# The end of an image-prompt cross-attention kernel, written out for its last two tiles

## The reference

```python
q = heads(hidden_states @ W_q)
probs_t = softmax(einsum(q, k_t) * attn_scale)
text_out = einsum(probs_t, v_t)
attn_scores = einsum(q, k_ip) * attn_scale
qsem = l2norm(einsum(probs_t, text_ehs))
sem = einsum(qsem, l2norm(ip_ehs))
fused = attn_scores + 0.5 * sem
probs_ip = softmax(fused) * spatial_mask
out = (text_out + einsum(probs_ip, v_ip)) @ W_out + b_out + hidden_states
```

## Time and profile before

| what | value |
|---|---|
| median of 3 runs | 332.41 us (332.4 to 334.32) |
| span of the profiled execution, first to last instruction | 330.6 us |
| PE busy | 307.7 us (93%) |
| DVE busy | 285.0 us (86%) |
| ACT busy | 278.2 us (84%) |
| POOL busy | 208.3 us (63%) |

### The profile page before, as it was taken

The page is one execution under the profiler, slowest core; times in us unless marked ns, Lnnn a source line. Parts: engine busy times, 40 slices in busy tenths (PEclk is TensorE's granted clock), DMA queues, the critical chain, the costliest instruction groups (busy, mean ns, idle before and its releaser), DMA issues.

```text
span 330.6 us, 9014 instructions
## 1 busy us (share of the span) xinstructions
PE 307.7 (93%) x2290; PEld 290.9 (88%) x2290; DVE 285.0 (86%) x1966; ACT 278.2 (84%) x1210; POOL 208.3 (63%) x422
## 2 busy tenths in 40 slices
PE   3999899898999999999999999999999999999974
PEld 3788878798999899989999999989998999899863
DVE  5666757899899989999999989998999899989973
ACT  3836688989999898989898989898989989898941
POOL 3053326686958686767776777768786967664241
PEclk9999999999999999999999999999999999999999
DMA  6960003001202020202011020212021201000001
GB/s 200 343 179 0 1 13 82 3 1 32 60 22 63 29 64 20 63 27 59 27 28 42 25 61 22 60 34 60 22 61 33 61 21 62 30 22 21 23 21 61
DMA packets 15131, 17.02 MB, mean 51 GB/s; under 512 B 2592, under 2 KB 14536, under 8 KB 15080
## 3 DMA queue, kind: packets, MB, share of 16 engines
q1 hardware_dynamic: 15080, 16.44, 16.5%
HBM read 10.55 MB, written 5.24 MB: 48 GB/s over the span
## 4 chain that ended last, share of the span: by engine, by line
PE 48%; DVE 24%; ACT 24%; issue 2%; DMA 1%; SPq 0%
PE gv_ps L902 13%; ACT e_sb L528 12%; PE mi_ps L865 9%; DVE place_ctxT L682 7%; PE mi_ps L937 7%; PE et_ps L889 6%; PE sc_ps L881 5%; DVE negmax L674 3%; ACT place_w L541 2%; DVE attnT_low L759 2%; ACT xh L504 2%; DVE q_rest L662 2%; DVE qs L665 2%; ACT place_ctxT L537 2%; ACT xh L506 2%
## 5 line engine op out<-in xcount | busy, mean ns | idle before, releaser
L528 ACT ACTIVATE e_sb<-sc_ps,negmax 128x60 f32<-128x60 f32 x640 | 150.2, 339 | 16.1 <-DVE negmax L674 15.2
L902 PE MATMUL gv_ps<-tab,place_w 128*128 128x162 f32 x640 | 115.1, 302 | 0.6 <-ACT place_ctxT L537 0.6
L682 DVE CUSTOM_DVE_ANT_0 place_ctxT<-gv_ps,e_sb 128x60 f32<-128x60 f32 x640 | 99.7, 210 | 13.8 <-PE gv_ps L902 11.7
L902 PEld LDWEIGHTS gv_ps<-tab,place_w 128*128 128x128 f32 x640 | 94.0, 190 | 1.8 <-issue 1.0
L881 PE MATMUL sc_ps<-km,qs 128*128 128x256 f32 x320 | 77.4, 324 | 0.0
L889 PE MATMUL et_ps<-ident,e_sb 128*128 128x128 f32 x320 | 63.2, 279 | 8.8 <-ACT e_sb L528 8.0
L541 ACT COPY place_w<-et_ps 128x256 f32<-128x256 f32 x160 | 66.5, 416 | 0.3 <-PE et_ps L889 0.3
L674 DVE TENSOR_REDUCE negmax<-sc_ps 128x4 f32<-128x240 f32 x160 | 63.2, 395 | 0.0
L889 PEld LDWEIGHTS et_ps<-ident,e_sb 128*128 128x128 f32 x320 | 40.9, 139 | 18.3 <-ACT e_sb L528 16.9
L682 DVE DVE_READ_ACCUMULATOR2_ANT quad<- 128x1 f32 x640 | 51.7, 81 | 0.0
L537 ACT COPY place_ctxT<-gv_ps 128x84 f32<-128x84 f32 x160 | 43.7, 273 | 6.5 <-DVE quad L682 6.4
(11 more groups left out here) (158 smaller groups left out, 583.5 us busy)
## 6 DMA issues: line engine op xcount, KB each, us to landing
x_nat<-in_x SPq DMA_DIRECT2D x16, 320.0 KB, 3.1
out<-place_w SPq DMA_DIRECT2D x32, 160.0 KB, 1.8
place_ctx<-in_ctx SPq DMA_DIRECT2D x4, 256.0 KB, 4.0
place_w<-in_L_xattn_W_v SPq DMA_DIRECT2D x1, 640.0 KB, 7.3
place_w<-in_L_xattn_W_k SPq DMA_DIRECT2D x1, 640.0 KB, 8.6
place_w<-in_L_xattn_W_k_ip SPq DMA_DIRECT2D x1, 640.0 KB, 10.3
place_w<-in_L_xattn_W_v_ip SPq DMA_DIRECT2D x1, 640.0 KB, 10.4
place_ctxT<-in_L_xattn_W_out SPq DMA_DIRECT2D x1, 640.0 KB
```

The costliest lines, as they stand in the source:

```text
L528: last = nc.scalar.activation(e_sb[:, slot, TOK * j:TOK * j + T], sc_ps[:, bank, TOK * j:TOK * j + T], ACT.Exp, bias=negmax[:, slot, j:j + 1])
L682: last = v.tensor_tensor_reduce(out=junk[:, u % 2, j, 0:T], in0=gv_ps[:, u % 2, TABW * j:TABW * j + T], in1=e_sb[:, u % ERING, TOK * j:TOK ...
L902: last = mm(gv_ps[:, u % 2, 2 * TABW * r:2 * TABW * r + 2 * TABW], eT[:, u % TRING, P * r:P * r + P], tab[:, b % 2, h:h + 2, :].rearrange( ...
```

## The change

What it does, part by part. A constant `PLAIN` (30) is the first of two tiles whose small steps leave the slots:

1. For tiles 30 and 31 `rnorm` is made on POOL with a power of -0.5 (128x20) ahead of the text part of `mixed`, in place of the logarithm and exponential on ACT.
2. For these tiles `semn`, `fused`, the maximum and `ipd` are a straight piece of DVE code, `centre(t)`: after slot 157 for tile 30, and after the last slot for tile 31. Sum, reciprocal and weighing are another, `normalize_and_weigh(t)`, after slot 158 and at the end. The weighing is one DVE instruction (`weigh`) in place of two on POOL, for tile 29 too. ACT's `ipe` of tile 30 stands after slot 157, that of tile 31 at the end.
3. `ENDING` puts the transposes of tile 29 in slot 158 (from 159) and its products in 159 (161), those of tile 30 in 160 (164) and 161 (166). Tile 31's text transposes come right after slot 160.
4. The image-prompt chunk of tile 31 is copied in fp32 and multiplied in one fp32 product, in place of a rounded half, a remainder and three fp32r products.
5. The residuals of tiles 29 and 30 are added at the end of DVE's program, after `xl`, the remainder of tile 31's text chunks.

```diff
+    PLAIN = ALL_TILES - 2
+        ENDING = {-2: ("at", -3), -1: ("o", -3), 0: ("at", -2), 1: ("o", -2)}
         def misc_task(u):
+            if u >= ALL_UNITS - 2:
+                kind, t = ENDING.get(u - ALL_UNITS, ("", 0))
+                return kind, 0, ALL_TILES + t
...
@@ GpSimd, tile(t)
+                if PLAIN <= t - 1 < ALL_TILES:
+                    pool.wait_ge(quadc_made, t)
+                    g.tensor_tensor(rnorm[:, b1], quadc[:, b1], neg_half[:], ALU.pow).then_inc(rnorm_made, 1)
                 if 0 <= t - 1 < ALL_TILES:
                     pool.wait_ge(rsum_made, t)
                     g.tensor_tensor(mixed[:, (t - 1) % ARING, 0:C].rearrange("p (h d) -> p h d", d=D), fin[:, b1, :, NIP:NIP + D],
...
-                if 0 <= t - 2 < ALL_TILES:
+                if 0 <= t - 2 < PLAIN - 1:
                     pool.wait_ge(iprec_made, t - 1)
...
-                if 0 <= t - 1 < ALL_TILES:
+                if 0 <= t - 1 < PLAIN:
                     pool.wait_ge(rnorm_made, t)
...
@@ ScalarE
+            def weights(t):
+                act.wait_ge(ipd_made, t + 1)
+                nc.scalar.activation(ipe[:, t % 2], ipd[:, t % 2], ACT.Exp).then_inc(ipe_made, 1)
-            for u in range(ALL_UNITS + GROUPS + 1):
+            for u in range(ALL_UNITS + 2):
                 slot(u)
+                if u == ALL_UNITS - 3:
+                    weights(PLAIN)
+            weights(PLAIN + 1)
             act.wait_ge(last_done, 1)
             nc.scalar.copy(last_attnT[:, 0:2 * P], LAST_ATTN[:, 0:2 * P]).then_inc(last_hi, 1)
             act.wait_ge(last_done, 2)
-            nc.scalar.copy(last_attnT[:, 2 * P:3 * P], LAST_IP).then_inc(last_hi, 1)
+            nc.scalar.copy(last_ip[:], LAST_IP).then_inc(last_hi, 1)
...
@@ VectorE
+                    if t - 2 == PLAIN - 1:
+                        weigh(t - 2)
...
+            def weigh(t):
+                dve.wait_ge(iprec_made, t + 1)
+                v.scalar_tensor_tensor(
+                    out=mixed[:, t % ARING, C:C + IPCOLS].rearrange("p (h n) -> p h n", n=NDIF), in0=ipe[:, t % 2, :, 0:NDIF],
+                    scalar=mask_sb[:, t % TILES:t % TILES + 1], in1=iprec[:, t % 2].unsqueeze(2).to_broadcast([P, HEADS, NDIF]),
+                    op0=ALU.mult, op1=ALU.mult).then_inc(pip_made, 1)
+            def centre(t):
+                n, steps = t % 2, 3 * (t - PLAIN)
+                dve.wait_ge(fin_copied, GROUPS * (t + 1))
...
+                dve.wait_ge(guard_made, t + 1)
+                v.tensor_tensor(quadc[:, n], quad[:, n], guard[:, n], ALU.max).then_inc(quadc_made, 1)
+                v.reciprocal(rsum[:, n], ssum).then_inc(rsum_made, 1)
+                dve.wait_ge(rnorm_made, t + 1)
+                v.tensor_tensor(semn[:, n], fin[:, n, :, 0:NIP], rnorm[:, n].unsqueeze(2).to_broadcast([P, HEADS, NIP]),
+                                ALU.mult).then_inc(end_step, 1)
...
+            def normalize_and_weigh(t):
+                n = t % 2
+                dve.wait_ge(ipe_made, t + 1)
...
+            for u in range(ALL_UNITS + 1):
                 slot(u)
+                if u == ALL_UNITS - 3:
+                    centre(PLAIN)
+                if u == ALL_UNITS - 2:
+                    normalize_and_weigh(PLAIN)
+            centre(PLAIN + 1)
+            attnT_lows(PLAIN)
+            normalize_and_weigh(PLAIN + 1)
             dve.wait_ge(last_hi, 1)
...
-            dve.wait_ge(last_hi, 2)
-            v.tensor_tensor(last_attnT_low[:, 2 * P:3 * P], LAST_IP, last_attnT[:, 2 * P:3 * P].bitcast(F32),
-                            ALU.subtract).then_inc(last_lo, 1)
+            for t in (PLAIN - 1, PLAIN):
+                add_residual(mi_ps[:, misc_bank(("o", 0, t)), 0:C], t)
             add_residual(LAST_OUT, ALL_TILES - 1)
@@ TensorE, last_products and the loop
-                pe.wait_ge(last_lo, 2)
-                for k in range(len(steps) - 3, len(steps)):
-                    last = mm(LAST_OUT, steps[k][0], steps[k][1], start=False, stop=k == len(steps) - 1)
-                last.then_inc(out_done, 1)
+                pe.wait_ge(last_hi, 2)
+                mm(LAST_OUT, last_ip[0:OUT_ROWS], u_nat[0:OUT_ROWS, B - 1], start=False, stop=True).then_inc(out_done, 1)
+            for u in range(ALL_UNITS + 1):
                 slot(u)
+            last_attn_transposes()
+            slot(ALL_UNITS + 1)
+            slot(ALL_UNITS + 2)
             last_products()
```

More of the change, by code:

```diff
@@ L268, in xattn_kernel @@
         MISC_ORDER = [("x", 0, 0), ("x", 1, 0), ("q", 0, 0), ("q", 1, 0), ("q", 2, 0), ("v", 0, 0), ("x", 0, 1), ("x", 1, 1)]
-        MISC_ORDER += [misc_task(u) for u in range(ALL_UNITS + UNITS) if misc_task(u)[0]]
+        MISC_ORDER += [misc_task(u) for u in range(ALL_UNITS + GROUPS) if misc_task(u)[0]]
         def misc_bank(task):
@@ L489, in tile @@
                                     ALU.subtract).then_inc(ipd_made, 1)
-            for t in range(ALL_TILES + 2):
+            for t in range(ALL_TILES + 1):
                 tile(t)
@@ L613, in slot @@
                     exps(u + LEAD)
-                if j == 3 and 0 <= t - 1 < ALL_TILES:
+                if j == 3 and 0 <= t - 1 < PLAIN:
                     act.wait_ge(lnq_made, t)
@@ L618, in slot @@
                     copy_eT(u + TLEAD)
-                if j == 0 and 0 <= t - 2 < ALL_TILES:
+                if j == 0 and 0 <= t - 2 < PLAIN:
                     act.wait_ge(ipd_made, t - 1)
@@ new lines, in centre @@
+            def centre(t):
+                n, steps = t % 2, 3 * (t - PLAIN)
+                dve.wait_ge(fin_copied, GROUPS * (t + 1))
+                ssum = fin[:, n, :, FINW - 1]
+                v.scalar_tensor_tensor(out=guard[:, n], in0=ssum, scalar=EPS * EPS, in1=ssum,
+                                       op0=ALU.mult, op1=ALU.mult).then_inc(guard_made, 1)
+                dve.wait_ge(guard_made, t + 1)
[4 more added lines that the diff above has]
+                                ALU.mult).then_inc(end_step, 1)
+                dve.wait_ge(end_step, steps + 1)
+                v.tensor_tensor(fused[:, n], semn[:, n], sip[:, t % SRING], ALU.add).then_inc(end_step, 1)
+                dve.wait_ge(end_step, steps + 2)
+                v.tensor_reduce(ipmax[:, n], fused[:, n], AX_X, ALU.max).then_inc(end_step, 1)
+                dve.wait_ge(end_step, steps + 3)
+                v.tensor_tensor(ipd[:, n], fused[:, n], ipmax[:, n].unsqueeze(2).to_broadcast([P, HEADS, NIP]),
+                                ALU.subtract).then_inc(ipd_made, 1)
@@ new lines, in normalize_and_weigh @@
+            def normalize_and_weigh(t):
+                n = t % 2
+                dve.wait_ge(ipe_made, t + 1)
+                v.tensor_reduce(ipsum[:, n], ipe[:, n], AX_X, ALU.add).then_inc(ipsum_made, 1)
+                dve.wait_ge(ipsum_made, t + 1)
+                v.reciprocal(iprec[:, n], ipsum[:, n]).then_inc(iprec_made, 1)
+                weigh(t)
+            for u in range(ALL_UNITS + 1):
+                slot(u)
+                if u == ALL_UNITS - 3:
+                    centre(PLAIN)
+                if u == ALL_UNITS - 2:
+                    normalize_and_weigh(PLAIN)
@@ L1087, in slot @@
                     table_products(u)
-            for u in range(ALL_UNITS + 2 * GROUPS - 2):
-                if u == ALL_UNITS + GROUPS + 1:
-                    last_attn_transposes()
+            for u in range(ALL_UNITS + 1):
                 slot(u)
+            last_attn_transposes()
+            slot(ALL_UNITS + 1)
+            slot(ALL_UNITS + 2)
             last_products()
```

10 lines of the change are left out of this document (5 added, 5 removed).

## The result

The changed kernel takes 346.86 us (median of 4 runs, 346.37 to 348.71) against 333.37 us for the kernel before in the same comparison: a ratio of 1.0426, 95% interval 1.039 to 1.0463. It is slower, as forecast, but by 13.5 us where 6.1 were forecast; it lies above the range.

The account below looks back on a forecast made before the run. The prediction took the end to be bound by the order in which engines wait for each other, none being full: 5.0 us up to quad(159) plus 1.1 after it, 332.4 + 6.1 = 338.5 us, range 334 to 344.

Parts of the forecast that it names:

- one power: POOL's 128x20 power for `rnorm`, tiles 30 and 31: taken as 1.2 us each, between bounds 0.59 and 7.4.
- end of power to end of `semn`: DVE's `semn` ends 0.14 us after POOL's 0.74 us text multiplication: 0.88 us after the power, instead of about 0.24.
- end of `semn` to end of `ipd`: `fused`, the maximum and `ipd` on DVE with their self-waits: 0.73 us in the sum.
- quad(156) to quad(159): DVE, ACT and PE queues stop at tile 30's power; quad(159) ends at 324.44, 5.0 us later than before.
- quad(159) to the last residual: Tile 31's small steps, then tile 30's products and the last chunk: 9.99 us against 8.92, 1.07 later.
- whole end, over before: Both parts of the end, before and after quad(159): 5.0 + 1.1 = 6.1 us longer.
- The order of the waits: DVE waits at `semn`, ACT at `ipe`, PE for fin(156); tile 30's products wait for tile 29's residual.
- The hold: POOL's text multiplication slows DVE's `semn` beside it: 0.64 us, counted twice, 1.28 in the sum.
- The first rival: The power is paid by the column: 342 us at 3 us each, 351 at 7.4; power above 3 us, chance 0.10.
- The second rival: The power is short and POOL's multiplication doesn't hold `semn`: 335.5 to 337.2 us, chance 0.13.
- The fp32 product: Tile 31's last chunk: one 0.78 us product replaces three taking 0.72 and a remainder; saves 0.29 us.
- The third rival: At DVE's wait for `rnorm`, little is held and shorter steps decide: 331.6 us; not slower or smaller costs, chance 0.15.

Follow-up runs that it names:

- e2b: Changed kernel plus useless TensorE transposes (40, 8, 36 and 18 at four places in the end) to keep TensorE busy; 343.26 us, ratio 1.029.
- e3: Changed kernel with tile 29's residual moved into tile 31's centering, in VectorE's wait for the power; 345.31 us, ratio 1.0357.
- e6: Changed kernel with POOL's `mixed` of both last tiles waiting for `ipd`, so it can't run beside `semn`; 346.24 us in one run.
- e1: Changed kernel without the power: ScalarE makes `rnorm` for the last two tiles by logarithm and exponential; 342.42 us, ratio 1.0243.
- e9: e1 plus useless TensorE transposes (12, 8, 8 and 16 at four places in the end); 337.25 us, ratio 1.0105.
- e8: Kernel before with one fp32 last-chunk product, tiles 30 and 31 weighed on VectorE, three neighbours exchanged; no power; 330.93 us, ratio 0.9913.
- e10: e9 with e3's move, POOL's `mixed` of tile 30 held until `ipd`, 6 transposes instead of 16 before tile 30's products; 334.52 us, ratio 1.0032.
- e2: Changed kernel plus useless TensorE transposes (34, 24 and 12 at three places in the end); 344.39 us, ratio 1.0328.

## Why the prediction was wrong, and where it was right

Its steps against the rows. Predicted lengths are from the text above; e2b is the changed kernel at an undiminished clock.

| step | predicted, us | changed kernel | e2b |
|---|---|---|---|
| one power | 1.2 | 3.57 and 3.54 | 3.57 and 3.54 |
| end of power to end of `semn` | 0.88 | 0.82 and 0.80 | |
| end of `semn` to end of `ipd` | 0.73 | 0.81 | |
| quad(156) to quad(159) | 8.24 | 12.27 | 10.67 |
| quad(159) to the last residual | 9.99 | 13.62 | 12.32 |
| whole end, over before | +6.1 | +13.74 | +10.84 |

**The order of the waits was right.** DVE stood at `semn`, ACT at `ipe` with fin(156) behind it, PE at gv(158), quad(159) came late, and tile 30's products waited for the residual of tile 29 (2.29 us, and 1.58 us of the time by e3).

**The hold was right.** It was put at 0.64 us and is 0.54 by e6. The rule of the Trainium skill that the prediction weighed (Advanced Engine Details and Errata, GPSIMD Details: a shared interface, and conflicts with VectorE instructions that read two SBUF inputs) agrees with e6: 0.78 against 0.24 us for the same instruction.

**The power was the wrong term.** The prediction bounded it between 0.59 us (all start-up) and 7.4 (all by the column) and took 1.2, "on the low side", since the only row was near the low end. That row could not say which: it had a single column, so its nearness to the low bound was a result of the size it was taken at, and no evidence. It is 0.39 us of start-up and 0.157 a column. Two times 2.36 us more (3.56 - 1.2) turn the predicted +6.1 into +10.8, and e2b, where the clock is full, measures +10.84; both of its partial lengths agree as well (8.24 + 2.36 = 10.60, measured 10.67; 9.99 + 2.36 = 12.35, measured 12.32). That it agrees to 0.1 us is luck in part: e2b's median stands 10.03 us over the kernel before in its comparison (343.26 against 333.23). The first rival, "paid by the column", had this mechanism and got a chance of 0.10. At 3.56 us it gives 332.4 + 10.8 = 343.2 us, so this miss alone would have left the time inside the range. The second rival falls: the power was not short, and the hold was there.

**The clock was a term that was missing.** The windows of before show 1.00 all through the earlier trace rows, and the sum priced every product by rows at that level, although its own account had PE idle from gv(157) to gv(158). After, PE stood still for 5.17 us there, and the clock fell; the nine products of tile 30 took 2.74 us where the earlier trace rows, from which they were priced, has 1.59. It cost 2.90 us (after against e2b); in the pair without the power it cost 19.54 - 16.32 = 3.22 (e1 against e9), so even with no power at all the term was missing. Power and clock together took the time out of the range. The Trainium skill (TensorE: Matmul & The Clock Gate, Part 1) states that an idle TensorE goes to the lower of two rates. The traces here agree (0.50 after the idle time), and that rule should have been set against the predicted idle time.

**The fp32 product** was put at a gain of 0.29 us. From the start of the last chunk's copy to the start of the last residual it went from 1.39 to 1.16 (340.90 to 342.06, the same in e8): 0.23.

**The third rival** (the time doesn't rise) was to decide at a wait of DVE for `rnorm` under 0.8 us; the wait is 3.50. But a wait below it doesn't suffice: in e9 it is 0.35, and the end is still 4.17 us longer, because the written-out order puts tile 30's softmax ahead of the work of units 157 to 159, tile 29's products ahead of gv(159), and tile 29's residual behind tile 31's steps. `semn` itself is shorter on DVE, as this rival had it: 0.24 us in e6 against 0.34. But the rival was priced without what stands behind the wait in the queues.

The 13.74 us are then 6.67 for the powers, 2.90 for the clock, 1.88 for the residual of tile 29 and the hold of tile 30 (e9 against e10), and 2.29 for the rest of the order. By the medians, each against the kernel before in its own comparison, the same four are 6.0, 3.5, 2.5 and 1.6, so which of the last two is the larger stays open.

Two slips in the prediction's text move nothing: its steps from `fused` to `ipd` add up to 0.72 us and enter the sum as 0.73, and five POOL instructions go per tile, not six.

## What to carry to other kernels

An operation whose only row has one column has no known price at twenty: split it into start-up and rate by one run at two sizes, or forecast over the whole span between the bounds. When a prediction makes TensorE wait for microseconds, price the products behind the wait at the lower clock too, and ask whether some harmless work can fill the wait. And a serial chain that is written out in an engine's strict order is paid for by everything behind it: here the written-out order, with the power and the clock taken out, made the end 4.17 us longer.

## What the runs showed of the hardware that was not expected

GpSimd's power took 1.169, 1.952 and 3.520 us at 5, 10 and 20 columns (a multiplication of 320 columns takes 0.744), and the number of partitions didn't matter: 3.520 on 32, 3.57 and 3.54 on 128 (about 4.6 in the one that ran beside two-operand VectorE work).

The granted clock fell to 0.50 after idle times of TensorE of 5.17 us (changed kernel), and fell too after two of 1.82 and 1.46 close together (e1) and one of 2.24 (e2), while it stayed at 1.00 in the runs whose longest idle time there was 1.21 (the kernel before), 0.92 (e2b), 0.80 (e9), 0.66 (e10) and 0.53 (e8). Two of 1.46 in e2, the first behind 34 transposes, left it at 1.00 too. Filling the idle time with useless transposes made two kernels faster, by 2.90 and 3.22 us at the end.
